# A transformer layer on one core: V projected in rows for two heads, query blocks between the score steps, attention written without loops

## What is computed

```
x  = L0_attn_x                                   # (2, 1024, 256)
xn = _layernorm(x, axis=-1)
# attention, 16 heads of 128, causal
q = (xn @ Wq + bq).reshape(b, h, t, dh)          # head-major view of the rows: no transpose
k = (xn @ Wk + bk).reshape(b, t, h, dh).transpose(0, 2, 3, 1)
v = (xn @ Wv + bv).reshape(b, t, h, dh).transpose(0, 2, 1, 3)
logits  = jnp.einsum('bhtd,bhds->bhts', q, k) * scale
weights = jax.nn.softmax(logits + mask, axis=-1)
out = jnp.einsum('bhts,bhsd->bhtd', weights, v)
out = out.transpose(0, 2, 1, 3).reshape(b, t, h * dh) @ Wo + bo
# feed-forward, 2048 wide, weights unpacked from 4-bit codes and scales
gate = xn @ Wg.T ; up = xn @ Wu.T
inter = gelu_tanh(gate) * up
return x + out + inter @ Wd.T
```

## Time and profile before

| | us |
|---|---|
| median of 3 runs | 1382.64 |
| lowest and highest run | 1381.21 and 1383.4 |
| span of the profiled execution | 1378.4 |
| PE busy in it | 1301.3 (94%) |
| DVE busy | 960.6 (70%) |
| ACT busy | 802.6 (58%) |
| POOL busy | 792.9 (58%) |

### The profile page before, as it was taken

One profiled execution on the slowest core, in us unless ns is written; L12 is line 12 of the kernel. 1 busy time (PEld: TensorE's weight loads), 2 busy tenths in 40 slices (PEclk: granted clock), 3 DMA queues, 4 the chain that ended last, 5 costly groups with the idle time before them and its releaser, 6 DMA issues.

```text
span 1378.4 us, 25462 instructions
## 1 busy us (share of the span) xinstructions
PE 1301.3 (94%) x7628; PEld 1091.0 (79%) x7628; DVE 960.6 (70%) x1489; ACT 802.6 (58%) x1720; POOL 792.9 (58%) x799
## 2 busy tenths in 40 slices
PE   3899999998989999999999999999999999999996
PEld 2677777776668888878888887788888868888885
DVE  7777778887756666677665767766666686676665
ACT  3556555555366666645666665466666636666663
POOL 5566666666065576543656675266655715566563
PEclk9899999999999999999999999999999999999999
DMA  4000000000200000011000001100000020000003
GB/s 94 14 7 12 13 11 11 11 26 0 81 15 19 18 11 12 11 54 31 12 11 23 11 11 30 53 11 11 11 19 15 11 61 12 22 11 11 11 23 122
DMA packets 68144, 33.07 MB, mean 24 GB/s; under 512 B 17552, under 2 KB 68112, under 8 KB 68112
## 3 DMA queue, kind: packets, MB, share of 16 engines
q10 hardware_dynamic: 42544, 23.01, 5.8%
q1 hardware_dynamic: 25568, 9.66, 2.7%
HBM read 30.57 MB, written 2.10 MB: 24 GB/s over the span
## 4 chain that ended last, share of the span: by engine, by line
PE 68%; DVE 2%; issue 2%; ACT 1%; POOL 1%; DMA 1%; ACTq 0%; DVEq 0%; POOLq 0%
PE ps L43 19%; PE ps L45 18%; PE ps L44 18%; PE ps L1106 9%; PE ps L1045 2%; PE ps L1096 1%; DVE q_all L933 1%; DMA q_all<-in_x 1%; DVE neg_max L989 0%; POOL probs L878 0%; DVE v_lo L906 0%; DVE wq_lo L917 0%; POOL inv_sum L874 0%; POOL q_lo L854 0%; ACT pt_hi L781 0%
## 5 line engine op out<-in xcount | busy, mean ns | idle before, releaser
L951 DVE TENSOR_TENSOR pt_lo<-ps,pt_hi 128x512 fp32r<-128x512 f32 (+3 forms) x384 | 204.0, 552 | 275.4 <-ACT pt_hi L781 272.8
L874 POOL TENSOR_TENSOR inv_sum<-row_sum,minus_one 128x1 f32<-128x1 f32 x256 | 141.5, 553 | 379.2 <-ACT probs L795 379.2
L878 POOL TENSOR_TENSOR probs<-probs,inv_sum 128x128 f32<-128x128 f32 (+7 forms) x256 | 294.1, 1149 | 20.0
L795 ACT ACTIVATE probs<-ps,neg_max 128x128 f32<-128x128 f32 (+7 forms) x256 | 190.1, 743 | 115.7 <-DVE neg_max L989 111.6
L989 DVE TENSOR_REDUCE neg_max<-ps 128x1 f32<-128x128 f32 (+7 forms) x256 | 191.8, 749 | 4.6 <-PE ps L1096 2.4
L781 ACT ACTIVATE pt_hi<-ps 128x512 fp32r<-128x512 f32 (+3 forms) x384 | 173.4, 488 | 34.9 <-PE ps L1106 34.8
L44 PE MATMUL ps<-pt_lo,v_hi 128*128 128x256 f32 (+1 forms) x640 | 177.6, 278 | 0.0
L45 PE MATMUL ps<-pt_hi,v_lo 128*128 128x256 f32 (+1 forms) x640 | 177.6, 277 | 0.0
L43 PE MATMUL ps<-pt_hi,v_hi 128*128 128x256 f32 (+1 forms) x640 | 173.8, 272 | 0.7 <-DVE pt_lo L951 0.7
L1106 PE MATMUL ps<-ident,probs 128*128 128x128 f32 x1152 | 171.0, 275 | 1.6 <-POOL probs L878 0.6
L43 PE MATMUL ps<-k_hi,q_hi 128*128 128x512 f32 (+3 forms) x384 | 142.7, 372 | 2.6 <-DVE q_lo L942 2.2
(11 more groups left out here) (106 smaller groups left out, 3140.5 us busy)
## 6 DMA issues: line engine op xcount, KB each, us to landing
wq_in<-in_wq ACTq DMA_DIRECT2D x67, 128.0 KB, 2.2
kv_in<-in_wk ACTq DMA_DIRECT2D x33, 128.0 KB, 2.3
kv_in<-in_wv ACTq DMA_DIRECT2D x33, 128.0 KB, 2.2
wo_in<-in_wo ACTq DMA_DIRECT2D x33, 128.0 KB, 2.0
q_all<-in_x SPq DMA_DIRECT2D x1, 2048.0 KB, 8.8
out<-q_all SPq DMA_DIRECT2D x8, 256.0 KB, 2.3
raw<-in_gate SPq DMA_DIRECT2D x18, 64.0 KB, 1.8
raw<-in_up SPq DMA_DIRECT2D x18, 64.0 KB, 1.9
```

The costliest lines, as they stand in the source:

```text
L795: nc.scalar.activation(probs[:, t % 4, 0:width], flat(S[t % 2])[:, 0:width], ACT.Exp, bias=neg_max[:, t:t + 1], accum_out=row_sum[:, t:t + ...
L874: nc.gpsimd.tensor_tensor(inv_sum[:, t:t + 1], row_sum[:, t:t + 1], minus_one[:], ALU.pow).then_inc(inv_done, 1)
L878: nc.gpsimd.tensor_tensor(row, row, inv_sum[:, t:t + 1].to_broadcast([P, (i + 1) * P]), ALU.mult).then_inc(probs_done, 1)
L951: nc.vector.tensor_tensor(pt_lo[where], T[at % 2][:, 0:blocks * P].rearrange("p (a b) -> p a b", b=P), pt_hi[where].bitcast(F32), ALU.subt ...
```

## The change

Attention is written out without hardware loops, all counts as constants. Within it:

- **V in rows, two heads at once.** A V job takes 256 rows of x as the stationary operand (two tiles) and the Wv columns of two heads as the moving one, so the result has rows of V for both heads: 12 matmuls of 256 columns. Vt0, Vt1 and `v_t` are gone. Two V jobs a head are left, Va behind `with_v` of step 3 and Vb ahead of the scores of step 7; V has three slots instead of two.
- **Weights.** Wk is loaded, split and kept for two heads, Wv in a tile of its own (`vw_in`, `vw_hi`, `vw_lo`). SP issues all loads in a fixed order; ACT issues none.
- **The next group's Q** is made in the last head of a group: eight `q_step`s of two blocks, behind steps 2 to 6 (`Q_AFTER`). A `q_step` takes one of the two score double banks in turn with the score tiles (`USERS`, `bank_free`).
- **The first group start** has four jobs between its eight `q_step`s instead of six jobs.
- **The 33rd head** and the last split of q are left out. `q_lo(0)` of a new group comes from POOL, not DVE.

The core of the diff:

```diff
-def load_kv(eng, sh, d, head):
-
-    cols = bass.ds((head & (HEADS - 1)) * DH, DH)
-    for part, name in enumerate(("wk", "wv")):
-        eng.dma_start(sh["kv_in"][:, :, part * DH:(part + 1) * DH],
-                      d[name].rearrange("(c p) n -> p c n", p=P)[:, :, cols]).then_inc(sh["kv_loaded"], 16)
+def load_kv(eng, sh, d, pair):
+
+    cols = slice(pair % (HEADS // 2) * 2 * DH, (pair % (HEADS // 2) + 1) * 2 * DH)
+    eng.dma_start(sh["kv_in"][:], d["wk"].rearrange("(c p) n -> p c n", p=P)[:, :, cols]).then_inc(sh["kv_loaded"], 16)
...
-        v_hi, v_lo = (sb(name, [P, 2, TILES, DH], F32R) for name in ("v_hi", "v_lo"))
-        v_t = sb("v_t", [P, 2, N], F32)
+        v_hi, v_lo = (sb(name, [P, VSLOTS, TILES, DH], F32R) for name in ("v_hi", "v_lo"))
...
-        JOBS = ["K0", "K1", "V0", "O0a", "O0b", "V1", "Vt0", "O1a", "O1b", "Vt1"]
-        ON_SCALAR = ["K0", "K1", "V0", "V1", "Vt0", "Vt1"]
-        ON_VECTOR = ["K0", "K1", "O0a", "O0b", "Vt0", "O1a", "O1b", "Vt1"]
-
-        FIRST_AT = {0: "K0", 2: "O0a", 6: "O1b", 7: "Vt1"}
+        FIRST_AT = {0: "K0", 2: "O0a", 6: "O1b", 7: "Vb"}
         EARLY_AT = {1: "K1", 3: "O0b", 5: "O1a"}
-        LATE_AT = {1: "V0", 3: "V1", 4: "Vt0"}
+        LATE_AT = {3: "Va"}
+        AT = [FIRST_AT[0], EARLY_AT[1], FIRST_AT[2], EARLY_AT[3], LATE_AT[3], EARLY_AT[5], FIRST_AT[6], FIRST_AT[7]]
         EAGER = (1, 3, 7)
-        FIRST_JOBS = ON_SCALAR
-        OUTPUTS = ["O0a", "O0b", "O1a", "O1b"]
+        Q_AFTER = {2: (0,), 3: (1,), 4: (2, 3), 5: (4, 5), 6: (6, 7)}
+        START = {0: ("K", 0, 1), 2: ("V", 0, 0), 4: ("V", 0, 1)}
...
+        def job_of(h, name):
+
+            if name is None:
+                return None
+            if name[0] == "K":
+                return ("K", h + 1, int(name[1])) if h + 1 < NH else None
+            if name[0] == "V":
+                pair, j = (h + 1) // 2, (0 if h % 2 else 2) + "ab".index(name[1])
+                return ("V", pair, j) if pair < NH // 2 else None
+            return ("O", h - 1, int(name[1]), "ab".index(name[2])) if h > 0 else None
...
+        new_group = lambda h: h % GROUP == GROUP - 1 and h + 1 < NH
+        q_steps = lambda h, i: Q_AFTER.get(i, ()) if new_group(h) else ()
+        eager = lambda h, i: i in EAGER or len(q_steps(h, i)) > 1
+
+        USERS = [("Q", 0, u) for u in range(8)]
+        for h in range(NH):
+            for i in range(TILES):
+                USERS.append(("S", h, i))
+                USERS += [("Q", h // GROUP + 1, u) for u in q_steps(h, i)]
+        place = {user: k for k, user in enumerate(USERS)}
...
+            def load_vw(pair):
+                sp.wait_ge(vw_lo_done, pair) if pair else None
+                for h in (2 * pair, 2 * pair + 1):
+                    cols = slice(h % HEADS * DH, (h % HEADS + 1) * DH)
+                    side = v_side(h)
+                    sp.dma_start(vw_in[:, :, side * DH:(side + 1) * DH],
+                                 d["wv"].rearrange("(c p) n -> p c n", p=P)[:, :, cols]).then_inc(vw_loaded, 16)
+
+            def load_wo(h):
+                sp.wait_ge(wo_lo_done, h) if h else None
+                rows = slice(h % HEADS * DH, (h % HEADS + 1) * DH)
+                sp.dma_start(wo_in[:], d["wo"][rows, :]).then_inc(wo_loaded, 16)
+
+            def load_q_block(n):
+                wait(sp, wq_lo_done, n - LOADS + 1)
+                load_wq(sp, sh, d, n, n % LOADS)
+
+            def load_kw(pair):
+                sp.wait_ge(kv_lo_done, pair)
+                load_kv(sp, sh, d, pair)
+
+            load_q_block(WQ_AHEAD)
+            load_vw(0)
+            load_wo(0)
+            load_kw(1)
+            for n in range(WQ_AHEAD + 1, HEADS + LOADS):
+                load_q_block(n)
+                if n == 8:
+                    load_vw(1)
+            for h in range(NH):
+                if h % 2 == 1 and (h + 3) // 2 < NH // 2:
+                    load_vw((h + 3) // 2)
+                if h + 1 < NH:
+                    load_wo(h + 1)
+                if new_group(h):
+                    o = h // GROUP + 1
+                    for n in range(o * HEADS + LOADS, min((o + 1) * HEADS + LOADS, GROUPS * HEADS)):
+                        load_q_block(n)
+                if h % 2 == 0 and h // 2 + 2 < NH // 2:
+                    load_kw(h // 2 + 2)
+
+            sp.wait_ge(q_lo_done, 2 * NH)
...
+            def q_ahead(o, u):
+
+                for n in (2 * u + 2, 2 * u + 3):
+                    if n < HEADS:
+                        wq_high(o * HEADS + n)
...
+            def q_step(o, u):
+
+                for n in (2 * u + 2, 2 * u + 3):
+                    if n < HEADS:
+                        wq_low(o * HEADS + n)
+                if u == 0:
+                    wait(dve, q_lo_done, 2 * GROUP * o)
+                for v in range(2):
+                    n = 2 * u + v
+                    dve.wait_ge(qp_done, o * HEADS + n + 1)
+                    dst = q_all[:].rearrange("p m r c -> p (m r) c")[:, :, n:n + 1]
                     nc.vector.tensor_scalar(
-                        dst.rearrange("p a b -> p (a b)"), S[u % 2][:, 0, :], bq[:, bass.ds(before + u, 1)],
+                        dst.rearrange("p a b -> p (a b)"), S[place[("Q", o, u)] % 2][:, v, :], bq[:, n:n + 1],
                         SCALE, ALU.add, ALU.mult).then_inc(q_done, 1)
...
+            def bank_free(user):
+
+                if place[user] < 2:
+                    return
+                kind, a, b = USERS[place[user] - 2]
+                if kind == "S":
+                    pe.wait_ge(exp_done, a * TILES + b + 1)
+                else:
+                    pe.wait_ge(q_done, a * HEADS + 2 * b + 2)
...
+            def project_v(pair, j):
+
+                pe.wait_ge(vw_lo_done, pair + 1)
+                for t in range(2):
+                    first = pair * 2 // HEADS * SEQ + (2 * j + t) * P
+                    rows = slice(first, first + P)
+                    for ch in range(KC):
+                        last = split_matmul(nc, M[:, t * 2 * DH:(t + 1) * 2 * DH], xn_hi[:, ch, rows],
+                                            xn_lo[:, ch, rows], vw_hi[:, ch, :], vw_lo[:, ch, :], ch == 0, ch == KC - 1)
                 return last
 
...
+            def q_step(o, u):
+                bank_free(("Q", o, u))
+                cols = slice(o * N, (o + 1) * N)
+                for v in range(2):
+                    n = o * HEADS + 2 * u + v
+                    pe.wait_ge(wq_lo_done, n + 1)
                     for ch in range(KC):
-                        last = split_matmul(nc, S[u % 2][:, 0, :], wq_hi[:, u, ch, :], wq_lo[:, u, ch, :],
-                                            xn_hi[:, ch, cols], xn_lo[:, ch, cols], ch == 0, ch == KC - 1)
+                        last = split_matmul(nc, S[place[("Q", o, u)] % 2][:, v, :], wq_hi[:, n % LOADS, ch, :],
+                                            wq_lo[:, n % LOADS, ch, :], xn_hi[:, ch, cols], xn_lo[:, ch, cols],
+                                            ch == 0, ch == KC - 1)
                     last.then_inc(qp_done, 1)
...
+            run(("K", 0, 0))
+            for u in range(8):
+                q_step(0, u)
+                run(START.get(u))
+
+            for s in range(NH * TILES):
+                h, i = divmod(s, TILES)
+                if s >= LAG:
+                    transposes(s - LAG)
+                run(job_of(h, FIRST_AT.get(i)))
+                scores(s)
+                run(job_of(h, EARLY_AT.get(i)))
+                if i % 2 == 1 and s >= LAG + 2:
+                    ph, pi = divmod(s - LAG - 2, TILES)
+                    with_v(ph, pi // 2)
+                run(job_of(h, LATE_AT.get(i)))
+                for u in q_steps(h, i):
+                    q_step(h // GROUP + 1, u)
+
...
```

More of the change, by code:

```diff
@@ L537, in attention @@
 def attention(nc, sh, d, out):
+    NH = BATCH * HEADS
     GROUP = N // (SEQ // HEADS)
[L551 to L552 removed]
+    GROUPS = NH // GROUP
     TILES = SEQ // P
@@ new lines, in pt_lows @@
+            def pt_lows(s):
+                for ch in range(banks_of(s % TILES)):
+                    pt_low(s, ch)
+            end = NH * TILES
+            pt_lows(end - 3)
+            o_low(NH - 1, 0)
+            add_residual(0)
+            add_residual(1)
+            evacuate(("O", NH - 1, 0, 0))
+            pt_lows(end - 2)
+            add_residual(2)
+            evacuate(("O", NH - 1, 0, 1))
+            pt_lows(end - 1)
+            add_residual(3)
+            add_residual(4)
@@ L1041, in project @@
                 return last
-            def v_rows(half):
-                for t in range(QT):
-                    last = nc.tensor.transpose(M[:, t * P:(t + 1) * P], v_t[:, half, t * P:(t + 1) * P], ident[:])
-                return last
-            def first_job(n):
-                job = FIRST_JOBS[n]
-                if n > 0 and FIRST_JOBS[n - 1] in ("V0", "V1"):
-                    pe.wait_ge(job_hi_done, n)
-                elif n > 0:
```

(31 more changed lines are left out.)

637 lines of the change are left out of this document (263 added, 374 removed).

## The result

| | before | after |
|---|---|---|
| median, us (4 runs each) | 1382.9 | 1334.05 |
| lowest and highest | 1381.21 and 1383.4 | 1333.19 and 1334.98 |
| span of the profiled execution | 1378.4 | 1333.0 |
| PE busy in it | 1301.3 | 1255.8 |
| instructions in it | 25462 | 21111 |

The ratio is 0.965, with a 95% interval from 0.9638 to 0.9662. The gain is 48.9 us, twice the 24.3 of the sum.

A forecast was written before the change was run, and what follows sets the result against it. Attention was taken to be bound by PE's instruction list. Steady heads -14.9, group changes +3.3, first scores -3.8, head 0 -1.5, last head -5.6 and drain -1.8 sum to -24.3 us: 1358.3 us, range 1343 to 1373.

The forecast's parts named there:

- Vt0: Steady head: removing its four transposes saves 0.44 us, of which 0.26 turns into a wait at O1a for Va's `v_lo`.
- Vt1: Steady head: nothing waits at its four transposes, so removing them saves their 0.35 us in full.
- Steady heads: 27 heads, each 0.55 us shorter, 14.9 in all; bounds nothing and the full 0.79 of both removed transpose blocks plus a tenth.
- the full gain: Sign in a steady head: 27.2 us from first scores to first scores would show all the removed transpose time gained.
- Group changes: Last head of a group with next Q inside: 56.05 us each against 54.88, +3.3 us for three; bounds 50.9 and 59.
- the walk through the waits: Group change: following the order with the rows' durations gave 6.2 us of PE waits on top of 49.85 us work.
- the 2 us of collisions: Group change: some 2 of the 6.2 us of waits, from Wq splits on DVE held up by POOL's product.
- Q blocks cost only themselves: Rival: group-change waits fall into each other, a change costs 50.9 us, 15.5 us less in all, 1343; chance 0.15.
- Head 0: V0 had waited 1.56 us for K1's k_lo; Va stands two steps later, so 1.5 us are saved.
- First scores: After the first group start: head 0's scores start at 378.5, 3.8 us earlier; bounds 2 and 5.
- Last head: Four projections and Vt0, Vt1 go, 6.4 us; transposes of tiles 6 and 7 wait 0.8, leaving 5.6; bounds 4 and 6.4.
- The drain: The load of x no longer waits for an unread split; O0b 2.0 us earlier, less 0.2 for pt_lo: 1.8 us.

The follow-up runs named there:

- run with four transposes: The changed kernel with four f32 transposes put back ahead of Vb, where Vt1 stood, in 30 heads: 1347.69 us.
- unrolled kernel before: The kernel before with every hardware loop of attention unrolled and all counts constants, nothing else changed: 1377.17 us.
- early order: The changed kernel with, in a group's last head, ACT's exponential of step 2 right behind its maximum and the first Wq roundings ahead of the exponential: 1325.38 us.
- a stretch made in the same way: The changed kernel with all eight `q_step`s put behind step 7 of the group's last head: 1329.95 us.
- A line moved: The changed kernel with `v_lo` of Va moved to the head of step 4 on DVE, ahead of pt_lo and o_lo: 1323.14 us.

## Why the prediction was wrong, point by point

**Steady heads, 0.94 in place of 0.55: the step that failed is the reading of what the removed work held, and "constants are worth nothing".**
- Vt1 was sized by the distance from its start to the next, 0.35. The run with four transposes shows 0.45: +0.10.
- Vt0: the wait that replaces part of it came where it was named, and at nearly the size (0.23 for 0.26). The removed part was again 0.45 by that run. Net 0.22 for 0.18.
- Straight code: 0.11 a head, which the prediction held at nothing because head 1, written out, took 28.12 and head 2, in the loop, 27.97. One head each was no test. Head 1 stands behind a half-filled head 0; its first block takes 0.16 us longer than that of a later head and the last transposes in it 0.1 longer, which hid the gain.
- This makes 0.45 + 0.22 + 0.11 = 0.78. The V jobs took back 0.07 (1.47 and 1.50 us for 1.45 each). So some 0.2 a head were not isolated by a run, and their cause stays open. The distances show where they are: the scores of step 7 take 1.43 behind a V job and took 1.51 behind Vt1, the transposes of tiles 6 and 7 take 0.03 less each, the first block of the head 0.04 less than in the unrolled kernel before, the product with V of step 1 and O0a together 0.05 less. Moving the loads off ACT is not it: that run left the heads at 27.06. A head of 27.06 is also below the 27.2 that the prediction had named as the full gain.

**Group changes, -2.2 in place of +1.1: the step that failed is the walk through the waits.** It gave 6.2 us of waits; measured are 52.69 - 27.06 - 22.35 = 3.3. The wait at the scores of step 3 was right (1.0 forecast, 0.93 in the row). The pairs of steps 4, 5 and 6 lost 1.3, 0.3 and 0.9 us, not 1.5, 1.0 and 1.5. The first `q_step` of step 6 lost nothing of its 0.65. (The losses in the steps add up to 3.7, since O1a, which waits in a steady head, does not wait here.) And the 2 us of collisions did not come. Timeline of DVE and POOL in step 5 of such a head:

```profile
594.90 0.76 DVE L883 TENSOR_TENSOR wq_lo<-wq_in,wq_hi 128x256 fp32r<-128x256 f32 x2 [1.37 <-ACT wq_hi L731]
...
594.64 0.55 POOL L839 TENSOR_TENSOR inv_sum<-row_sum,minus_one 128x1 f32<-128x1 f32 x1 [6.61 <-ACT probs L762]
595.27 1.72 POOL L842 TENSOR_TENSOR probs<-probs,inv_sum 128x768 f32<-128x768 f32 x1
```

The splits follow the exponential by one rounding of ACT, POOL's product follows it by `inv_sum`. So the splits come first, and it is the product that waits: 1.72 us, where the same width takes 1.47 in every other head, and PE needs it much later. Of the 48 splits in the three changes, three took 1.3 us (those behind step 1, beside POOL's `q_lo`) and 45 took some 0.42. Before, six of the 48 had taken 1.2 to 1.8, two in each group start: the change that was to bring more of these collisions has fewer. The Trainium skill (SBUF — State Buffer, "Who interferes with whom") has the exclusion of the two engines; the trace agrees, in both directions: 1.82 us for a split behind a product, 0.25 on a product behind a split. What the prediction lacked is the order of arrival. The rest of the 3.3 us between forecast and result, some 0.4, is the larger gain of the steady part of such a head.

The rival "Q blocks cost only themselves" named 50.9 us. The changed kernel went two thirds of the way to it from the forecast's 56.05; the early order reached and passed it (49.65). The comparison inside the forecast held: against a stretch made in the same way, Q between the steps did cost time (4.1 us). The old stretch had waits of its own, which the count of 4.5 us contained and which the new `q_step`s no longer have, wherever they stand.

**Head 0, -3.1 in place of -1.5.** The sum left out that head 0 loses its own Vt0 and Vt1, and counted one of its waits, not the second (Vt0 waited 1.00 us there for `v_t`). In four of the runs above head 0 had the full clock and took 19.1 to 19.3 us. That is not a gain of the whole, since in these four the stage ahead had ended 1.3 to 1.9 us later than in the changed kernel (last section).

**First scores** came as forecast (the first group start itself went from 35.6 to 31.5 us, and the stage ahead ended 0.4 later). **Last head**: the 5.6 us are partly luck. The wait ahead of the transposes of tile 6 was 1.44 us and not 0.8; O1a, which does not wait there, and the larger gain of the steady part made up for it. **The drain** gave 1.0, not 1.8: the wait for x is gone as said, but the clock fell (below). In the run with loads from ACT, whose drain kept the full clock to its last half microsecond, it takes 23.2 us, 2.2 less than before.

The chance of 0.15 for the only rival below 1358 was too low, but no rival had the steady heads at more than the full 0.79 plus a tenth; that bound was itself made from the distance 0.35.

## What to carry to other kernels

Size a removed step by taking its row and both neighbours together, from the start of the block ahead to the start of the block behind, and, where one can, by putting the step back. When a wait is left on the engine that bounds the kernel, look at the engine it waits for: if that one was idle just before, look at its order first and not at its load. A line moved can be worth nearly as much as a whole step removed (0.39 us a head here, against 0.45 for four transposes). Where two engines exclude each other, ask who arrives first; the later one pays, and it may be the one with time to spare.
